# Routed activation tiles turned as three full 128-column slices instead of four

## What is computed

```python
def step(acc, ew):
    w_gu, w_d, cw = ew
    h = _silu_mul(x @ w_gu.T, I)
    return (acc + h @ w_d.T * cw[:, None], None)
```

## Time and profile before

| | |
|---|---|
| median of three runs | 989.24 us |
| the profiled execution | 989.24 us, its span 987.4 us |
| TensorE busy | 888.0 us, 90% |
| VectorE | 701.0 us, 71% |
| ScalarE | 493.4 us, 50% |
| GpSimd | 480.5 us, 49% |
| mean granted TensorE clock | 0.974 of full |

### The profile page before, as it was taken

The page is one execution under the profiler, slowest core; times in us unless marked ns, Lnnn a source line. Parts: engine busy times, 40 slices in busy tenths (PEclk is TensorE's granted clock), DMA queues, the critical chain, the costliest instruction groups (busy, mean ns, idle before and its releaser), DMA issues.

```text
span 987.4 us, 20904 instructions
## 1 busy us (share of the span) xinstructions
PE 888.0 (90%) x6996; PEld 550.9 (56%) x6996; DVE 701.0 (71%) x1392; ACT 493.4 (50%) x865; POOL 480.5 (49%) x465
## 2 busy tenths in 40 slices
PE   2768889999938899899999989899999999999997
PEld 1355556666624666657665545454566445666564
DVE  6786524786789987735644898887879788875554
ACT  2856543577824577544755773344433553333322
POOL 3766267513586435277742888532433224422322
PEclk9978999999959999999999999999999999999999
DMA  9688545633121232957793542111110211112222
GB/s 304 258 220 173 122 132 124 130 77 81 61 75 64 76 72 72 223 199 138 174 191 117 159 142 85 59 52 54 43 54 23 78 50 48 54 45 87 71 69 64
DMA packets 123268, 106.63 MB, mean 108 GB/s; under 512 B 75672, under 2 KB 97944, under 8 KB 123168
## 3 DMA queue, kind: packets, MB, share of 16 engines
q1 hardware_dynamic: 117024, 88.51, 32.9%
q0 software_dynamic: 6144, 16.79, 5.9%
HBM read 58.98 MB, written 30.02 MB: 90 GB/s over the span
## 4 chain that ended last, share of the span: by engine, by line
PE 36%; DVE 5%; POOL 5%; issue 3%; ACT 1%; DMA 0%; POOLq 0%; DVEq 0%; SPq 0%; ACTq 0%
PE ps L1062 18%; PE ps L1111 9%; POOL wlo L771 2%; PE ps L1093 2%; PE ps L1037 2%; POOL hh L717 1%; POOL back L760 1%; PE ps L1255 1%; PE ps L1286 1%; PE ps L1275 1%; DVE hid L1329 1%; DVE scr L1660 1%; PE ps L1265 1%; PE ps L1079 1%; DVE hid L1337 1%
## 5 line engine op out<-in xcount | busy, mean ns | idle before, releaser
L717 POOL TENSOR_TENSOR hh<-hid,hh 128x512 f16<-128x512 f32 x120 | 144.6, 1205 | 256.0 <-ACT hh L828 255.6
L1323 DVE SCALAR_TENSOR_TENSOR hid<-gtanh,ps 128x512 f32<-128x512 f32 (+2 forms) x184 | 114.3, 621 | 153.2 <-ACT gtanh L808 150.6
L1062 PE MATMUL ps<-xhi,whi 128*128 128x512 f16 x480 | 184.5, 384 | 22.7 <-DVE hid L1323 18.5
L808 ACT ACTIVATE gtanh<-ps 128x512 f32<-128x512 f32 (+2 forms) x184 | 100.5, 546 | 193.5 <-PE ps L1062 158.3
L1062 PE MATMUL ps<-xlo,whi 128*128 128x512 f16 x480 | 184.2, 384 | 0.0
L1062 PE MATMUL ps<-xhi,wlo 128*128 128x512 f16 x480 | 184.0, 383 | 0.0
L1111 PE MATMUL ps<-whi,hh 128*128 128x256 f16 x960 | 176.3, 274 | 2.0 <-POOL hh L717 1.5
L1337 DVE SCALAR_TENSOR_TENSOR hid<-hid,ps 128x512 f32<-128x512 f32 (+2 forms) x184 | 114.4, 621 | 54.6 <-PE ps L1037 27.7
L1037 PE MATMUL ps<-whi,xs_sb 128*128 x992 | 127.9, 243 | 20.2 <-issue 13.5
L1111 PE MATMUL ps<-wlo,hh 128*128 128x256 f16 x480 | 131.4, 274 | 0.0
L828 ACT ACTIVATE hh<-hid 128x512 f16<-128x512 f32 x120 | 75.2, 627 | 110.1 <-DVE hid L1329 82.9
(11 more groups left out here) (208 smaller groups left out, 1579.5 us busy)
## 6 DMA issues: line engine op xcount, KB each, us to landing
ys_dram<-y_sb SPq DMA_DIRECT2D x60, 256.0 KB
xs_sb<-c_dram SPq DMA_DIRECT2D x64, 192.0 KB, 2.8
scr<-w_in SPq DMA_DIRECT2D x28, 384.0 KB, 4.3
scr<-we_in SPq DMA_DIRECT2D x32, 304.0 KB, 4.2
xs_sb<-c_dram SPq DMA_DIRECT2D x64, 128.0 KB, 3.0
xs_sb<-c_dram SPq DMA_DIRECT2D x64, 64.0 KB, 2.7
xs_dram<-y_sb SPq DMA_DIRECT2D x1, 3968.0 KB, 15.0
scr<-ws_in SPq DMA_DIRECT2D x8, 384.0 KB, 6.9
```

The lines of the kernel that those rows point to most:

```text
L717: pool.tensor_tensor(hlo[:, k, :], hid[:, k % 2, :], hhi[:, k, :], ALU.subtract).then_inc(lo_done, 1)
L808: act.activation(gtanh[:, n % 2, 0:w], ps[:, G_BANK, 0:w], ACT.Tanh, scale=0.5 / W_SCALE)\
L1062: mm = pe.matmul(ps[:, bank, :], w[:, off:off + P], a[:, kc, t0:t0 + HN], start=(i == 0), stop=(i == 3 * KC - 1))
L1323: dve.scalar_tensor_tensor(out=hid[:, k, 0:w], in0=gtanh[:, k, 0:w], scalar=1.0, in1=ps[:, G_BANK, 0:w], op0=ALU.add, op1=ALU.mult).then_i ...
```

## The change

The widths of the two parts become `IA` = 128 and `IB` = 48. `hp` gets 400 columns for each block: the high part (176), the low part (176) and a second copy of the high part's last 48 columns, written by a new ScalarE copy behind `hi`. The turn takes three slices of 128 columns, at 0, at 176 and at 272; the last one holds columns 96 to 175 of the low part and the 48 of the high tail. All five matmuls of a down use 128 rows. The weight tile of the tail has its rows at 32 to 79 and 80 to 127, and zeros in rows 0 to 31. A new semaphore `tail_done` is waited for by the turn and by the activation two units later. The constant `ones8` becomes a view of `onesf`, with one fill less on GpSimd. The strings of `ORDER` are new for all five engines; each holds the same steps as before in another order.

```diff
-IA = 112
+IA = P
 IB = I0 - IA
@@ ORDER: all strings of PE, ACT, DVE, POOL and SP; of PE the start
-        "s2 v2 s g2 s g4 d g2 d g2 v d g2 d g2 d g2 d g2 t g t d g t g d g2 t g d2 t g t g d2 g2 t v g2 d t g2 d "
...
-        ones8 = sb("ones8", [P, 8])
+        ones8 = onesf[:, 0:8]
...
-        hp = sb("hp", [P, 2, 2, 2, I0], F16)
+        hp = sb("hp", [P, 2, 2, 2 * I0 + IB], F16)
...
+        tail_done = sem("tail_done")
...
-            pool.memset(ones8[:, :], 1.0).then_inc(pool_consts, 1)
-            pool.wait_ge(pool_consts, 5)
+            pool.wait_ge(pool_consts, 4)
...
-                        pool.tensor_tensor(hp[:, j, 0:w, 1, 0:I0], hid[:, n % 2, 0:w * I0].rearrange("p (b i) -> p b i", i=I0),
-                                           hp[:, j, 0:w, 0, 0:I0], ALU.subtract).then_inc(lo_done, 1)
+                        pool.tensor_tensor(hp[:, j, 0:w, I0:2 * I0], hid[:, n % 2, 0:w * I0].rearrange("p (b i) -> p b i", i=I0),
+                                           hp[:, j, 0:w, 0:I0], ALU.subtract).then_inc(lo_done, 1)
...
-                        act.activation(hp[:, m % 2, 0:w, 0, 0:I0], hid[:, n % 2, 0:w * I0].rearrange("p (b i) -> p b i", i=I0),
-                                       ACT.Copy).then_inc(hi_done, 1)
+                        h = hid[:, n % 2, 0:w * I0].rearrange("p (b i) -> p b i", i=I0)
+                        act.activation(hp[:, m % 2, 0:w, 0:I0], h, ACT.Copy).then_inc(hi_done, 1)
+                        act.activation(hp[:, m % 2, 0:w, 2 * I0:2 * I0 + IB], h[:, :, IA:I0], ACT.Copy).then_inc(tail_done, 1)
...
                     pe.wait_ge(lo_done, n + 1)
+                    pe.wait_ge(tail_done, m + 1)
...
-                        for out, part in ((hT[:, at:at + P], hp[:, m % 2, b, 0, 0:P]),
-                                          (hT[:, at + P:at + 2 * P], hp[:, m % 2, b, 1, 0:P]),
-                                          (hT[0:IB, at + 2 * P:at + 3 * P], hp[:, m % 2, b, 0, IA:I0]),
-                                          (hT[IB:P, at + 2 * P:at + 3 * P], hp[:, m % 2, b, 1, IA:I0])):
-                            mm = pe.transpose(out, part, ident16[:, :])
+                        for i, col in enumerate((0, I0, 2 * I0 + IB - P)):
+                            mm = pe.transpose(hT[:, at + P * i:at + P * i + P], hp[:, m % 2, b, col:col + P], ident16[:, :])
...
-                                                                 (2, whi, P, D), (2, wlo, IB, D))):
+                                                                 (2, whi, P, D), (2, wlo, P, D))):
...
                         dve.wait_ge(lo_done, n - 1)
-
+                        r2, c2 = WHERE[n - 2]
+                        if PASSES[r2][0] == RT:
+                            dve.wait_ge(tail_done, BLOCK[r2] + c2 + 1)
...
-    we[:, 0:IA, 2 * KC * I0:2 * KC * I0 + D] = dn[:, 0:IA]
-    for at in (0, IB):
+    we[:, :, 2 * KC * I0:2 * KC * I0 + D] = dn[:, 0:IA]
+    for at in (P - IB, P - 2 * IB):
         we[:, at:at + IB, 2 * KC * I0 + D:] = dn[:, IA:]
```

More of the change, by code:

```diff
@@ L1390, in piece @@
                     e = E0 if n < 4 else E1
[L1391 removed]
+                    dve.wait_ge(pool_consts, 4)
                     dve.wait_ge(logits_ready, n + 1)
```

5 lines of the change are left out of this document (2 added, 3 removed), and 97 rows, old and new, of the table ORDER.

## The result

The changed kernel takes 982.9 us (median of 13 runs, 976.0 to 986.1), the kernel before 989.24 (13 runs, 985.1 to 991.8). The ratio is 0.993, 95% interval 0.991 to 0.995. So it gained 6.3 us where 23 were forecast. The profiled execution took 983.99 us with a span of 982.2.

The account below looks back on a forecast made before the run. In pure routed stretches TensorE's sequencer and array were taken as equally slow, among attention the array as the bound. Terms: -25.5 + 2.2 = -23.3; 987.4 + 1.8 - 23.3 = 965.9, so 966 us, range 944 to 984.

Parts of the forecast that it names:

- The price of a down and a turn: Per routed unit on TensorE: down 1.52 to 1.10 us, turn 0.79 to 0.34, together 0.86 us saved.
- How much of the 53 us the end sees: Of 53 us TensorE time saved in routed work, shares by stretch sum to 25.5 us, less 2.2 for the wait.
- three tenths: Share of 15.1 us taken in stretches 107 to 140 and 465 to 523 us, paced by the sequencer: 4.5 us.
- The wait on the tail: The turn's new semaphore wait costs TensorE's sequencer 0.13 us per unit where it paces: 2.2 us lost.
- Moved work, 0 with 4 us to either side: Rewriting the order of all five queues was taken to cost 0, with 4 us to either side.
- behind 540 us the same instructions run at the same prices: The part behind the routed work, 447 us long, was taken to stay as long as now.
- gates behind a down, 10 us old and 11 new: Routed gates waiting for the down four units before cost about 1.35 us where adjoining; new order loses 1 us.
- gaps stay: Rival: the down keeps its gaps because row count does not hold the load back; 978 us, chance 0.10.
- sequencer everywhere: Rival: the sequencer paces the attention stretches too, so 10 us gained; 979 us, chance 0.14.
- if the part behind 540 us moved by more than 4: Sign that the prediction is wrong: the stretch behind the routed work, 447 us long, changes by over 4 us.
- the forecast range of 4.4 to 4.7: Expected pace in us per routed unit in 465 to 523 us, against 5.0 before.

Follow-up runs that it names:

- full rows alone: The kernel before with all five down matmuls on 128 rows, four transposes, no tail copy and no new wait: 973.95 us, 0.984.
- the fixed experts: Experts fixed at build, no table reads or address calculations: kernel before 968.65 us; changed tiles with orders of before 946.0; changed kernel 964.76.
- the lock: Two combines moved on VectorE alone: 967.09 us where the new order behind the last routed pass took 973.7, and 976.38 where the changed kernel took 982.9.
- the 13 of the middle: Changed tiles, orders of before, but second to third routed pass with attention and norms in the new sequence: 978.01 us, 0.988, 13 over 964.65.
- the eased lock: Changed tiles with orders of before, one GpSimd subtraction and VectorE's router keep step each moved later: 964.5 us, 0.974.

## Why the prediction was wrong

*The price of a down and a turn:* right. 1.52 to 1.10 and 0.79 to 0.33, and the 26.4 us idle of the 64-row weight loads is gone. The run with full rows alone shows it to be the row count of the down, as the gaps in the earlier trace rows said. The rule of the Trainium skill, "TensorE: Matmul & The Clock Gate", section "LDWEIGHTS (loading the stationary operand)", that a load's time goes by its columns and not by its rows, does not cover this: the duration was nearly the same (93 ns against 98 for the loads of 128 rows), the start came late, and 15 us of the run were in that.

*How much of the 53 us the end sees:* the total of 23.3 was right, 24.6 measured. Its reasoning was partly right. I gave the pure routed passes three tenths because the sequencer paces them; the fixed experts show that the tiles gain as much without the sequencer's work. By passes the changed tiles gain, in the orders of before, 7.4 us until the end of the first routed pass, 5.9 in the second, 7.2 in the third, 4.8 in the last, and less than 1 us between and behind. The forecast's terms, put to the same passes with the wait's 2.2 taken off, give roughly 4, 7, 8 and 4. With a chance of a few us in each trace that does not tell the shares right from wrong: that the total came out is in part luck, since the reason given for one of them failed.

*The wait on the tail:* 2.2 us of loss predicted, nothing measured. The step's mistake is to add a semaphore's 0.13 us to the sequencer as if it had no slack; dropping the routed gates' waits gave 0.3 and 1.9 us, within the noise.

*Moved work, 0 with 4 us to either side:* this failed, by 18. It is the term that made the forecast wrong. Three steps of it were wrong. First, "behind 540 us the same instructions run at the same prices": VectorE's combine has no fixed price. It costs 0.48 us alone and 7.07 under a series of GpSimd, and which it is depends on the order. The earlier trace rows and the groups of the page, whose means mix both, don't tell that; the longest durations of a group would have. Second, TensorE's own matmuls have no fixed price either: the forecast has no term for the clock, and in the profiled execution TensorE is busy for 14.1 of the 20.1 us that the new orders add, with 80 us at half clock for 45. Third, I priced the order by one kind of place (gates behind a down, 10 us old and 11 new), and this kind is worth nothing in either kernel. In an order of 3,127 steps on five queues the places that decide were others, and I took the one that I could count for the whole. Of the 18 us 6.5 are shown by a test (the lock); for the 13 of the middle no single cause is shown. Since the order of before is itself written out step by step, a range of 4 us for another one had no row behind it: one stop such as the 2.9 us of the orders of before, moved in front of TensorE's operand, is already most of it.

*The rivals:* "gaps stay" gave 978 and "sequencer everywhere" 979, near the measured 982.9 by their number alone; neither is what happened. The gaps went, and the sequencer was not the cause. None of the rivals was a loss of this size by the order. The sign of it in the list of what would prove the prediction wrong, "if the part behind 540 us moved by more than 4", is the one that came: it is 456.6 for 447.4. The last routed down started at 525.6 where 516 was forecast and 514.8 is had with the orders of before; the pace of 4.6 us per unit (467.31 to 471.92) is in the forecast range of 4.4 to 4.7.

The version to keep is the changed tiles with the orders of before: 964.65 us, 0.977 [0.974, 0.980], 18 us below the changed kernel. Neither the dropped gate wait nor the eased lock adds anything measurable to it.

## What to carry to other kernels

When a change brings a new order along, forecast and measure the two apart: run the new code in the old order and the old code in the new one. For a new order, list each engine's longest instance of a group beside its median; an instruction that is at times ten times as long, as the combine here, is held up by something, and should not stand in front of the bottleneck's next operand. Compare the bottleneck's busy time of both traces before its waits: where the same instructions are busy for longer, the clock has a part in it. A weight load of fewer rows between loads of full rows can cost more than its duration says; look at the starts around it.

## What the runs showed of the hardware

- VectorE's instructions with both inputs in SBUF can be held for all of a back-to-back series of GpSimd: 0.48 us becomes 7.07 over five subtractions. In ten of 13 cases the wait went to the end of the series, in three only to the end of its first instruction. Instructions with one input in PSUM were not hit: in the changed tiles with the orders of before, line 1324 took 0.67 us at 598.80, in the middle of a series of GpSimd from 596.69 to 600.39.
- After a stop of 5.46 us TensorE's matmuls started 0.42 us apart instead of 0.22, at a granted clock of 0.50. With two combines moved 7.0 us came back in that stretch, 3.6 of them idle and 3.4 busy: a stop can cost more than its length.
- Another order of the same matmuls kept TensorE busy for 14.1 us longer (841.5 to 855.6), with 80 us at half clock for 45.
- Around weight loads of 64 rows among ones of 112 and 128, two matmuls started 0.10 us late, its own and the next; 128 rows for all of the down's gave 15 us (0.984 [0.981, 0.988]).
- TensorE's table reads and address calculations, 4.2 us per routed unit on its sequencer, are worth 18 to 24 us of the run in each of four kernels. Some of it is hidden in TensorE's busy time, which fell by 10.2 us in the kernel before (888.0 to 877.8) where the run fell by 20.6.
